# Folding the norms of self- and cross-attention into their projections, and projecting the values feature-major

## What is computed

```
x     = rms_norm(h, ln_in_w)                        # w * x * rsqrt(mean(x^2) + eps), over 256 features
mixed = where(vm, x @ v_qkv, x @ l_qkv)             # two experts, chosen per token
q, k, v = split(mixed, 3); q, k = rotary(q, k)      # 16 heads of 16
h     = h + where(vm, sdpa(q, k, v, causal) @ v_dense, ... @ l_dense)
ci    = rms_norm(h, ln_post_cross_w)
h     = h + sdpa(heads(ci @ cq_w), ck, cv) @ cdense_w   # 16 heads of 8; ck, cv from the context
mi    = rms_norm(h, ln_post_attn_w)
h     = h + where(vm, (silu(mi @ v_gate) * (mi @ v_up)) @ v_down, ... same with l_*)
```

## Time and profile before

| | |
|---|---|
| timed executions, median | 2611.38 us (2606.4 to 2613.58) |
| the profiled execution's own time | 2616.32 us |
| its span, first to last instruction | 2614.5 us |
| mean granted TensorE clock | 0.987 of full |
| busy: PE, DVE, ACT, POOL | 2498.3, 1508.3, 1221.4, 981.0 us |

### The profile page before, as it was taken

The page is one execution under the profiler, slowest core; times in us unless marked ns, Lnnn a source line. Parts: engine busy times, 40 slices in busy tenths (PEclk is TensorE's granted clock), DMA queues, the critical chain, the costliest instruction groups (busy, mean ns, idle before and its releaser), DMA issues.

```text
span 2614.5 us, 53886 instructions
## 1 busy us (share of the span) xinstructions
PE 2498.3 (96%) x20350; PEld 1496.2 (57%) x20350; DVE 1508.3 (58%) x3448; ACT 1221.4 (47%) x4274; POOL 981.0 (38%) x990
## 2 busy tenths in 40 slices
PE   6999989999999999999999999999999999999998
PEld 3546545655565655665555564666655556566565
DVE  2537547677444755766644474676654447467763
ACT  2335426446242644565524363556443347265462
POOL 0025345565110534555411151554531134256452
PEclk8999999999999999999999999999999999999999
DMA  7000022112210002111220101111121010210111
GB/s 204 1 29 10 15 71 59 30 55 57 73 50 25 10 4 63 50 42 37 78 61 14 33 2 38 42 37 54 31 87 60 1 33 2 61 52 16 54 42 58
DMA packets 156154, 113.81 MB, mean 44 GB/s; under 512 B 30804, under 2 KB 153464, under 8 KB 155768
## 3 DMA queue, kind: packets, MB, share of 16 engines
q1 hardware_dynamic: 151440, 110.04, 14.5%
q10 hardware_dynamic: 4456, 0.29, 0.2%
HBM read 101.87 MB, written 8.42 MB: 42 GB/s over the span
## 4 chain that ended last, share of the span: by engine, by line
PE 79%; DVE 12%; ACT 3%; issue 3%; POOL 2%; ACTq 1%; DMA 0%; DVEq 0%; SPq 0%; POOLq 0%
PE bank L1433 10%; PE bank L1450 6%; PE bank L1064 6%; PE bank L1150 5%; PE bank L1338 4%; PE bank L1326 4%; PE bank L1347 4%; PE bank L1319 4%; PE bank L1373 3%; PE bank L1439 2%; ACT Ebuf L1538 2%; PE bank L1126 2%; PE bank L1310 2%; PE bank L1299 2%; PE bank L1071 2%
## 5 line engine op out<-in xcount | busy, mean ns | idle before, releaser
L1936 POOL TENSOR_TENSOR Ebuf<-Ebuf,row_rcp 128x512 f32<-128x512 f32 (+1 forms) x328 | 344.1, 1056 | 832.5 <-DVE row_rcp L1759 830.7
L1538 ACT ACTIVATE Ebuf<-bank,minus_max 128x64 f32<-128x64 f32 x1312 | 392.3, 333 | 33.6 <-DVE minus_max L1743 32.1
L1538 ACT ACTIVATION_READ_ACCUMULATOR Ebuf<-bank,minus_max 128x1 f32 x1312 | 296.1, 226 | 0.0
L1743 DVE TENSOR_REDUCE minus_max<-bank 128x8 f32<-128x512 f32 (+1 forms) x328 | 219.2, 673 | 133.1 <-PE bank L1126 62.5
L1547 ACT ACTIVATE PT<-bank 128x512 f32<-128x512 f32 (+1 forms) x328 | 191.7, 610 | 121.9 <-PE bank L1150 120.7
L1150 PE MATMUL bank<-ident,Ebuf 128*128 128x128 f32 x1296 | 202.8, 284 | 13.5 <-POOL Ebuf L1936 10.5
L1150 PEld LDWEIGHTS bank<-ident,Ebuf 128*128 128x128 f32 x1296 | 148.1, 144 | 77.6 <-issue 50.9
L1433 PE MATMUL bank<-xs_b,w_ring 128*128 128x512 f32 (+1 forms) x384 | 172.1, 611 | 2.1 <-DVE xs_b L1829 2.1
L1433 PE MATMUL bank<-xs_a,w_ring 128*128 128x512 f32 (+1 forms) x384 | 172.3, 612 | 0.4
L1531 ACT ACTIVATE Ebuf<-Ebuf 128x512 f32<-128x512 f32 x160 | 101.7, 636 | 91.6 <-DVE Ebuf L1748 89.1
L1748 DVE TENSOR_TENSOR Ebuf<-bank,minus_max 128x512 f32<-128x512 f32 x160 | 110.7, 692 | 17.3 <-DVE minus_max L1743 0.5
(11 more groups left out here) (325 smaller groups left out, 5339.0 us busy)
## 6 DMA issues: line engine op xcount, KB each, us to landing
w_ring<-differences SPq DMA_DIRECT2D x70, 384.0 KB, 3.5
w_ring<-in_L_W SPq DMA_DIRECT2D x64, 256.0 KB, 3.0
w_ring<-in_L_l_gate SPq DMA_DIRECT2D x80, 128.0 KB, 3.4
w_ring<-in_L_l_up SPq DMA_DIRECT2D x80, 128.0 KB, 3.1
w_ring<-in_L_l_down SPq DMA_DIRECT2D x80, 128.0 KB, 3.1
differences<-w_ring SPq DMA_DIRECT2D x10, 384.0 KB, 2.8
arena_a<-in_x SPq DMA_DIRECT2D x4, 512.0 KB
arena_b<-in_x SPq DMA_DIRECT2D x4, 512.0 KB
```

The source lines that it names most:

```text
L1538: last = A(Ebuf[:, u % UNITS, cell], bank(token)[:, cell], ACT.Exp, bias=minus_max[:, u % UNITS, c:c + 1], accum_out=row_sum[:, u % UNITS, ...
L1743: V.reduce_max(minus_max[:, u % UNITS, 0:g], cells(bank(token)[:, 0:g * S]), AX_X, negate=True).then_inc(maxed, 1)
L1936: G_.tensor_tensor(v, v, row_rcp[:, n % 3, 0:g].unsqueeze(2).broadcast_to([P, g, S]), ALU.mult).then_inc(probs_ready, 1)
```

## The change

The gains of norms 3, 4, 6 and 7 are multiplied into the projection weights `w_qkv` and `w_cq` once, by POOL in `zero_s`. The projections then read the residual xT itself. The inverse root of each token, which the norm would have applied before the product, is applied after it: for keys and values by DVE when it takes the product from the bank (from `st.root`, the spread roots that ACT copies), for queries in the softmax, as a scale of the exponential (`query_scale`, a column with one value per token on the partitions); for odd units DVE multiplies the negated maxima by it too. So the maxima are taken of unscaled scores, and the causal mask is made smaller by 1e-4. The spread and the normed copy of norms 4 and 7 go away; norms 3 and 6 keep the spread. A new step `mask` makes xv from xT. The values are projected feature-major like `qk` (`vt`, twice), and `v` becomes 4 PE transposes, twice. Keys and queries swap places, so that queries come first. `LOADED` goes from 10 to 6. Lines of context, semaphores and bookkeeping of the planner are left out here:

```diff
@@ -99,12 +99,12 @@
-    steps = norm_steps(3 * n - 3, 0.0)
-    at = 9.0
+    steps = [(0.0, "mask", n)] + norm_steps(3 * n - 3, 0.0)
+    at = 1.0
-                                       ("rope", 1), ("rot", 2), ("v", 0), ("rot", 3), ("rope", 2), ("rope", 3), ("v", 1))):
+                                       ("rope", 1), ("rot", 2), ("vt", 0), ("rot", 3), ("rope", 2), ("rope", 3), ("vt", 1), ("v", 0), ("v", 1))):
-        at += {"qk": 2.1, "rot": 0.9, "rope": 0.01, "v": 3.5}[step]
+        at += {"qk": 2.1, "rot": 0.9, "rope": 0.01, "vt": 2.1, "v": 0.8}[step]
...
@@ -119,7 +119,7 @@
-        steps += [(at, "dense", n, h), *norm_steps(3 * n - 2, at + 1.2, h, 2.0), (at + 6.4, "cq", n, h)]
+        steps += [(at, "dense", n, h), *norm_steps(3 * n - 2, at + 1.2, h, 2.0)[:2], (at + 2.4, "cq", n, h)]
...
@@ -204,11 +204,12 @@
+FOLDED = (3, 6)
-              "qk", "v", "cv", "ck", "cq", "dense", "cdense", "g", "u", "out")
+              "qk", "vt", "v", "cv", "ck", "cq", "dense", "cdense", "g", "u", "out")
-LOADED = 10.0
+LOADED = 6.0
...
@@ -235,6 +236,10 @@
+    if step == "mask":
+        return [("DVE", 0.45, None), ("POOL", 2.15, None)]
+    if step == "spread" and n in FOLDED:
+        return chain(("PE", 0.45), ("ACT", 0.6))
...
@@ -256,8 +261,8 @@
-        "l1h": (("PE", 1.75), ("ACT", 0.55)), "w2": (("PE", 1.75),), "qk": (("PE", 2.2), ("ACT", 0.55)), "rope": (("DVE", 0.9),),
-        "v": (("PE", 3.45), ("ACT", 1.5)), "cv": (("PE", 1.05), ("ACT", 0.55)), "ck": (("PE", 0.9), ("ACT", 0.55)), "values": (("ACT", 0.8),),
+        "l1h": (("PE", 1.75), ("ACT", 0.55)), "w2": (("PE", 1.75),), "qk": (("PE", 2.2), ("DVE", 0.7) if where and where[-1] % 2 else ("ACT", 0.55)), "rope": (("DVE", 0.9),),
+        "vt": (("PE", 2.2), ("DVE", 0.7)), "v": (("PE", 0.45), ("ACT", 1.5)), "cv": (("PE", 1.05), ("ACT", 0.55)), "ck": (("PE", 0.9), ("ACT", 0.55)), "values": (("ACT", 0.8),),
...
@@ -345,6 +352,14 @@
+
+
+SCALED_BY_ROOT = ("self", "cross")
+
+
+def scale_of(key):
+
+    return (3 * key[1] - 3, 0) if key[0] == "self" else (3 * key[1] - 2, key[2] // 4)
...
@@ -712,6 +739,7 @@
+        st.root = st.xn[:, 0, :]
...
@@ -1354,24 +1392,30 @@
-                            ready_l = [xn_ready[s].at(turn, XN_AT[3 * n - 3] + k + 1) for k in range(DT)]
+                            ready_l = [res_done[s].at(turn, RES_AT[3 * n - 3] + k + 1) for k in range(DT)]
-                        at = (i // 2) * P + (D if i % 2 == 0 else 0)
+                        at = (i // 2) * P + (D if i % 2 else 0)
-                                [st.xn[:, k, :] for k in range(DT)], [st.xv[:, k, :] for k in range(DT)], every,
+                                [st.xT[:, k, :] for k in range(DT)], [st.xv[:, k, :] for k in range(DT)], every,
+                    if step == "vt":
+                        n, i = where
+                        b = fill(token)
+                        at = 2 * D + i * P
+                        experts(b[:, :], [w_qkv[n, "l"][:, k, at:at + P] for k in range(DT)],
+                                [w_qkv[n, "v"][:, k, at:at + P] for k in range(DT)],
+                                [st.xT[:, k, :] for k in range(DT)], [st.xv[:, k, :] for k in range(DT)], every).then_inc(full(token), 1)
-                        pe.wait_ge(*xv_early[s].at(turn, LATE_AT[3 * n - 3] + 1))
+                        pe.wait_ge(*emptied(("vt", s, turn, n, 1)))
-                            p = 2 * i + c
-                            for k, (e, src) in enumerate((e, src) for e, src in (("l", st.xn), ("v", st.xv)) for _ in range(DT)):
-                                last = mm(b[:, c * D:(c + 1) * D], src[:, k % DT, p * P:(p + 1) * P],
-                                          w_qkv[n, e][:, k % DT, 2 * D:3 * D], start=(k == 0), stop=(k == 3))
+                            for m in range(DT):
+                                p = 2 * i + c
+                                last = nc.tensor.transpose(b[:, c * D + m * P:c * D + (m + 1) * P], v_turned[:, m, p * P:(p + 1) * P], ident[:, :])
...
@@ -1401,9 +1445,9 @@
-                        pe.wait_ge(*xn_ready[s].at(turn, XN_AT[3 * n - 2] + 2 * h + DT))
+                        pe.wait_ge(*emptied(("dense", s, turn, n, h)))
-                            last = mm(b[:, 0:HALF], w_cq[n][:, k, :], st.xn[:, k, span(4, h)], start=(k == 0), stop=(k == DT - 1))
+                            last = mm(b[:, 0:HALF], w_cq[n][:, k, :], st.xT[:, k, span(4, h)], start=(k == 0), stop=(k == DT - 1))
...
@@ -1528,15 +1572,22 @@
-                        A(v, v, ACT.Exp).then_inc(exped, 1)
+                        if key[0] in SCALED_BY_ROOT:
+                            act.wait_ge(*rstd_ready[s].at(turn, RUN[scale_of(key)] + 1))
+                            A(v, v, ACT.Exp, scale=query_scale(st, key)).then_inc(exped, 1)
+                        else:
+                            A(v, v, ACT.Exp).then_inc(exped, 1)
-                    act.wait_ge(maxed, u + 1)
+                    if key[0] in SCALED_BY_ROOT:
+                        act.wait_ge(scaled, SCALED[s, turn, key] + 1)
+                    else:
+                        act.wait_ge(maxed, u + 1)
-                                 accum_out=row_sum[:, u % UNITS, c:c + 1])
+                                 scale=query_scale(st, key) if key[0] in SCALED_BY_ROOT else 1.0, accum_out=row_sum[:, u % UNITS, c:c + 1])
...
@@ -1593,11 +1644,16 @@
+                if step == "spread":
+                    if where[0] == 6:
+                        act.wait_ge(*xv_early[s].at(turn, LATE_AT[6]))
+                    act.wait_ge(*filled(token))
+                    A(st.root, bank(token)[:, :], ACT.Copy).then_inc(root_ready[s].sem, 1)
-                    A(st.qk[:, where[1], :], bank(token)[:, :], ACT.Copy).then_inc(qk_ready[s].sem, 1)
+                    A(st.qk[:, slot(where[1]), :], bank(token)[:, :], ACT.Copy).then_inc(q_ready[s].sem, 1)
...
@@ -1686,7 +1742,7 @@
-                    V.tensor_copy(causal_bf[:, :], Ebuf[:, 0, 0:S]).then_inc(s_setup, 1)
+                    V.tensor_scalar(causal_bf[:, :], Ebuf[:, 0, 0:S], 1e-4, None, ALU.mult).then_inc(s_setup, 1)
...
@@ -1747,6 +1803,11 @@
+                    elif key[0] in SCALED_BY_ROOT:
+                        dve.wait_ge(maxed, u + 1)
+                        dve.wait_ge(*rstd_ready[s].at(turn, RUN[scale_of(key)] + 1))
+                        V.tensor_scalar(minus_max[:, u % UNITS, 0:g], minus_max[:, u % UNITS, 0:g], query_scale(st, key), None, ALU.mult
+                                        ).then_inc(scaled, 1)
...
@@ -1805,13 +1866,25 @@
+                if step == "mask":
+                    norm = 3 * where[0] - 3
+                    if norm == 3:
+                        dve.wait_ge(*masks_ready[s].at(turn, 1))
+                    dve.wait_ge(*res_done[s].at(turn, RES_AT[norm] + DT))
+                    V.tensor_tensor(late(st.xv), late(st.xT), late(both(st.is_v)), ALU.mult).then_inc(xv_late[s].sem, 1)
+                if step == "qk":
+                    if where == [3, 1]:
+                        dve.wait_ge(*hv_early[s].at(turn, FT))
+                    dve.wait_ge(*root_ready[s].at(turn, where[0] - 1))
+                    dve.wait_ge(*filled(token))
+                    V.tensor_tensor(st.qk[:, slot(where[1]), :], bank(token)[:, :], st.root, ALU.mult).then_inc(k_ready[s].sem, 1)
+                if step == "vt":
+                    dve.wait_ge(*root_ready[s].at(turn, where[0] - 1))
+                    dve.wait_ge(*filled(token))
+                    V.tensor_tensor(v_turned[:, where[1], :], bank(token)[:, :], st.root, ALU.mult).then_inc(vt_ready[s].sem, 1)
-                    if n == 3:
-                        dve.wait_ge(*masks_ready[s].at(turn, 1))
-                    if n == 6:
-                        dve.wait_ge(*xv_early[s].at(turn, LATE_AT[6]))
...
@@ -1849,6 +1922,8 @@
+                        if i == 0:
+                            dve.wait_ge(*xv_early[s].at(turn, LATE_AT[3 * n - 3] + 1))
...
@@ -1940,10 +2015,27 @@
+                            pool.wait_ge(s_tiled, 16 * len(GAINS))
+                            for k in range(DT):
+                                G_.tensor_scalar(w_cq[n][:, k, :], w_cq[n][:, k, :], norm_gain(3 * n - 2, k), None, ALU.mult)
+                                for e in "lv":
+                                    w = w_qkv[n, e][:, k, :]
+                                    last = G_.tensor_scalar(w, w, norm_gain(3 * n - 3, k), None, ALU.mult)
+                            last.then_inc(w_scaled, 1)
+                            pool.wait_ge(w_scaled, n - 1)
+                if step == "mask":
+                    norm = 3 * where[0] - 3
+                    if norm == 3:
+                        pool.wait_ge(*masks_ready[s].at(turn, 1))
+                    pool.wait_ge(*res_done[s].at(turn, RES_AT[norm] + DT))
+                    for m in range(DT):
+                        v, x = (by_batch(some[:, m, :])[:, :, 0:LATE] for some in (st.xv, st.xT))
```

(23 more changed lines are left out.)

51 lines of the change are left out of this document (31 added, 20 removed).

## The result

The changed kernel takes 2654.5 us (2647.5 to 2655.2, four executions) where the kernel before, on the same chip, takes 2608.9 (2606.4 to 2613.6). The ratio is 1.0167 [1.0142, 1.0191]: slower, where 2564 was forecast. The range, 2525 to 2612, does not hold it. The profiled execution took 2647.5 us; it is the fastest of the four (granted clock 0.984, the others 0.979), so the page shows 31.2 of the difference.

The account below looks back on a forecast made before the run. PE was taken to bound the kernel, with work in 93% of a middle turn. Terms -24.9 - 9 - 14 - 25 + 10 + 15 = -47.9 took the profiled 2616.3 to 2568.4, less 4.9 is 2564 us; range 2525 to 2612.

Parts of the forecast that it names:

- the softmax's term, +15: Odd attention units: DVE operation and scale operand delay exponentials; one in eight of 120 us reaches PE, bounds 0 and +60.
- the softmax becomes the bound of attention: Rival: odd units' eight exponentials on ACT run late and PE runs out of work; 2632 us at 70% exposed, chance 0.17.
- another rival: Only the work on PE is won: the holes move, waits and entries give 0; 2602 us, chance 0.17.
- The scaling's term, +10: POOL's one-time weight scaling in `zero_s`: 5.9 to 15.7 us, taken as +10, all landing on PE.
- Values, -24.9: Both `v` steps of a stage become `vt` steps and transposes, 6.91 to 5.36 us; 16 stages, bounds -23 to -27.
- a microsecond of PE work taken away is worth nearly a microsecond: Opening step on PE: 597.7 us of a 640 us turn are work, so removed PE work comes off the time.
- Spreads and their waits, -9 and -14: Norms 4 and 7 on PE: 32 spread steps removed, -9; idle ahead of 18 of them, 19.2 us, three quarters won.
- The entry, -25: Residual to first `qk` matmul, 16 stretches: `qk` and `vt` fill two thirds of 38.3 us without work.
- the banks' rival: At the entry, keys and values hold banks awaiting the root, so PE stops for banks; 2612 us, chance 0.06.
- DVE and `LOADED`, 0: DVE's extra microsecond per stage is hidden, and `LOADED` moves only planned places; both counted at 0.
- the likeliest case: The forecast itself, 2564 us, chance 0.48, spanning 2545 to 2595 with the softmax and scaling terms varied.

## Why the prediction was wrong

**The step that failed most is the softmax's term, +15.** Its price was right: 88 ns for the operand, where 92 were read off the tanh; DVE's small operation was 0.35 to 0.43 us, not 0.20. But I took the exposed share, one in eight, from waits of an order that had been written for the old duration. In it the operand costs time to seven tenths (70 of 98.6 us), in the kernel before to six (56 of 92.3); once the planner knows it, to three tenths (29 of 92.2) and less than one (6.5 of 89.9). This is the rival "the softmax becomes the bound of attention", held at 0.17 and priced at a share of 70%, half right in its cause: the same exponentials cost 29 us once the order expects them. The time came out above its 2632, as the gains it set against the loss were smaller. I had used "costs that do not know the operand's price" as an argument for another rival, where it belonged here.

**The scaling's term, +10,** was mis-sized. POOL's scaling of 768 columns takes 2.2 us, more per column than the product of two tiles that I had as the upper bound: 20.4 us in place of 5.9 to 15.7. Where it would land was right, PE's wait at 159 us. Moving it away, with the differences behind it, wins 15, 16 and 23 us (three pairs by ratio). GPSIMD Engine Reference (section "Engine selection") of the Trainium skill has operations of one input near the line rate; for this one the trace differs, 2.9 ns a column against 2.2 for the two-input product.

**Values, -24.9.** The work went as said and more: from start to follower the `v` steps took 112.1 us before; after, the 32 `vt` steps take 67.6 (the 96 steps of this shape 209.4, 64 before 141.8) and the turns 14.9: 29.6 us less. The step that failed is the sentence ahead of it, "a microsecond of PE work taken away is worth nearly a microsecond". Alone, the part is worth about 1 us on the mean of three orders. PE's 93% of work in a turn did not show what that work waits for: 30.0 of the 33.5 us come back, by the count above nearly all as dummies and as waits for the turned values and POOL's product. That a chain through DVE, ACT and POOL bounds a turn is argued, not shown; the chain that ended last is 77% PE in that run, 79% before.

**Spreads and their waits, -9 and -14.** Right in the trace: the half spreads go from 23.8 to 9.3 us, from start to follower, 14.5 less where I took 9, and no wait is left ahead of norms 4 and 7. What both are worth in time was not measured apart.

**The entry, -25,** was half right. `qk` comes at once, as said, and the banks' rival did not come: no wait for a bank that a key holds is among the long ones. But time without work over 30 us behind the residual falls only from 44.5 to 33.3 us, 11 and not 25. The run without the operand and with the scaling early has 35.9 in the same windows, so this is not the operand's doing. As I read it, the `vt` steps that fill the entry are missing later, when rotary, keys and values pass through DVE; that rests on the one place shown.

**DVE and `LOADED`, 0.** `LOADED` was right within what orders scatter. DVE was not free: the turns wait 8.4 us for it.

The sum by runs: 2609 - 49.6 (values, spreads, waits, entry) + 23 (scaling) + 70 (operand) = 2652. The three steps lead from run to run up to the changed kernel, so the sum comes out by itself and proves nothing; it shows the sizes. By the prediction's terms the same three were -72.9, +10 and +15. (Three of the prediction's figures are a rounding off: values -24.8, the likeliest case 2544 to 2594.) Open stays how the 49.6 divide among the four parts in the presence of each other, and what would have to move for the values' part to be won.

## What to carry to other kernels

An order written out at build time holds for the durations it was written with: when an edit makes an instruction dearer, raise its cost in the planner in the same edit, and do not price the edit untold at the share of waits that the old order shows: here six and seven tenths of its time on a side engine reached the end. Do not read a busy share of 93% as a price for work taken away; do the part alone, and do it in two or three orders, since a new order of the same work moved these kernels by up to 19 us down and 14 up. Setup work that stands in a queue in front of a critical product belongs where that engine idles.

## What the runs showed of the hardware

A scaling by a column on POOL (128x768, 2.20 us) costs more per column than a product of two tiles (128x1536, 3.42 us). A multiplication of 128x8 on DVE took 0.34 us by a constant and 0.35 to 0.43 by a column, where a reciprocal of that shape takes 0.20; so the column is not the main part of its length. The second operand of an exponential slows the pace of eight in a row as much as the single one, 0.30 to 0.39 us.
